# Four gated attention layers: shared expert in loops, no padding chunks, one dispatch buffer filled ahead, loads of SyncE reordered

## The reference

```python
x = x + tanh(g_xattn[l]) * attention_l(layernorm(x), ctx, ctx)
x = x + tanh(g_ffn[l]) * ffn_l(layernorm(x))   # layers 0 to 3
```

## Time and profile before

| | us |
|---|---|
| median of 3 runs | 2857.65 |
| lowest and highest of them | 2852.08, 2864.13 |
| the profiled execution | 2859.82 |
| its span in the trace | 2858.0 |

### The profile page before, as it was taken

The page is one execution under the profiler, slowest core; times in us unless marked ns, Lnnn a source line. Parts: engine busy times, 40 slices in busy tenths (PEclk is TensorE's granted clock), DMA queues, the critical chain, the costliest instruction groups (busy, mean ns, idle before and its releaser), DMA issues. The chain is left out here.

```text
span 2858.0 us, 66667 instructions
## 1 busy us (share of the span) xinstructions
PE 2314.3 (81%) x24114; PEld 1670.9 (58%) x24114; DVE 1598.7 (56%) x4258; ACT 1438.7 (50%) x2187; POOL 976.3 (34%) x1058
## 2 busy tenths in 40 slices
PE   6887774359999489889999998999969887159993
PEld 3554543249898255556777775555535554159982
DVE  5788886234444378852222222799968988413333
ACT  4665652123333277764454544777757666024441
POOL 4447774504444222211000000122112455734545
PEclk8999985679999799989999999999989999579996
DMA  3322221126666244430000000333313333157777
GB/s 87 104 76 82 77 84 52 38 74 207 203 206 180 81 119 118 117 91 13 0 0 0 0 0 1 94 103 103 109 56 91 95 104 95 59 161 218 231 219 229
DMA packets 183495, 284.19 MB, mean 99 GB/s; under 512 B 29177, under 2 KB 104449, under 8 KB 182722
## 3 DMA queue, kind: packets, MB, share of 16 engines
q1 hardware_dynamic: 119506, 122.36, 16.3%
q10 hardware_dynamic: 46480, 122.88, 13.1%
q0 software_dynamic: 17280, 35.95, 3.7%
HBM read 188.53 MB, written 76.91 MB: 93 GB/s over the span
## 5 line engine op out<-in xcount | busy, mean ns | idle before, releaser
L1798 DVE TENSOR_REDUCE mx<-psS 128x16 f32<-128x1024 f32 x264 | 322.2, 1221 | 197.5 <-PE psS L1297 190.3
L744 POOL DMA_INDIRECT yg<-ysb,yidx x284 | 276.1, 972 | 412.9 <-DVE ysb L2245 220.9
L1297 PE MATMUL psS<-kexp,qT 64*64 64x512 f32 x2112 | 297.2, 633 | 51.3 <-DVE work L1800 31.3
L1306 PEld LDWEIGHTS psT<-ident,work 128*128 128x128 f32 x2080 | 241.3, 147 | 166.3 <-ACT work L854 78.2
L854 ACT ACTIVATE work<-work 128x1024 f32<-128x1024 f32 x264 | 278.0, 1053 | 112.4 <-DVE work L1800 89.3
L860 ACT ACTIVATE work<-psT 128x1024 f32<-128x1024 f32 x260 | 265.4, 1021 | 127.3 <-PE psT L1306 122.0
L1800 DVE TENSOR_TENSOR work<-psS,mx 128x1024 f32<-128x1024 f32 x264 | 323.2, 1224 | 9.1
L1306 PE MATMUL psT<-ident,work 128*128 128x128 f32 x2080 | 291.4, 285 | 26.8 <-ACT work L854 12.9
L540 POOL TENSOR_TENSOR ve<-mv,eps 128x4 f32<-128x4 f32 x85 | 17.2, 202 | 818.0 <-DVE mv L1734 817.4
L1653 PEld LDWEIGHTS psY<-w_ffn,work 128*128 128x128 f32 x1988 | 243.9, 192 | 10.2 <-DVE work L2222 1.9
L1653 PE MATMUL psY<-w_ffn,work 128*128 128x128 f32 x1988 | 245.2, 275 | 2.0 <-DVE ysb L2245 1.4
(11 more groups left out here) (259 smaller groups left out, 4437.8 us busy)
## 6 DMA issues: line engine op xcount, KB each, us to landing
w_ffn<-in_wmoe ACTq DMA_DIRECT2D x71, 578.0 KB
w_ffn<-in_wmoe ACTq DMA_DIRECT2D x71, 576.0 KB
rawd<-raw ACTq DMA_DIRECT2D x64, 512.0 KB
vsum<-rawd SPq DMA_DIRECT2D x128, 256.0 KB
xin<-xg SPq DMA_DIRECT2D x142, 132.0 KB
ctxT<-in_ctxT SPq DMA_DIRECT2D x72, 256.0 KB
kexp<-kT SPq DMA_DIRECT2D x1144, 16.0 KB
gio<-yg SPq DMA_DIRECT2D x16, 512.0 KB, 6.0
```

The source lines that it names most:

```text
L744: e.indirect_dma_start(out=yg, out_offset=bass.IndirectOffsetOnAxis(ap=yidx[:, b, t:t + 1], axis=0), in_=ysb[:, b, t, :], in_offset=None, ...
L1297: m = e.matmul(psS[64 * half:64 * half + 64, 512 * k:512 * k + 512], qT[64 * k:64 * k + 64, b, c:c + SEQ], kexp[64 * k:64 * k + 64, b, :, ...
L1306: m = e.transpose(psT[:, r * P:(r + 1) * P], sc[:, s % 2, 2 * r:2 * r + 2, :].rearrange("p a b -> p (a b)"), ident[:, :])
L1798: e.tensor_reduce(mx[:, :], src, AX, ALU.max).then_inc(s_max, 1)
```

## The change

1. The shared expert runs as two chunks, a loop of six passes of two chunks, and two chunks, on PE, ACT and DVE. In the loop DVE's mean, scale and x slices have addresses from the loop register.
2. Chunks past the end are gone: NP, NK, NS and NT fall away, and a helper returns early.
3. `xg` is split in `xg[0]` and `xg[3]`. All regions of `xg[3]` are filled with padding rows by `prefill`, which SP issues behind barrier 3; the eight pad writes ahead of the experts of layer 3 are gone, and POOL waits for the fill before it scatters in attention 3. ACT's first 1056 KB pad write is made for each buffer.
4. On SP `y_load(None, 2)` of attention 1 stands ahead of `spread_k(1, None, 1)`; the 2048 KB weights of feed-forward 1 come in four loads, one behind each of the last four turns; `spread_k(1, None, 0)` moves from ahead of barrier 1 to the end of `experts(0)`.

```diff
+        def past(i, u):
+            return i is None and u >= CHUNKS
...
             def spread_k(lay, i, u):
+                if past(i, u):
+                    return
...
             def shift(lay, i, u, s):
+                if past(i, u):
+                    return
...
-                if lay in (0, 1):
-                    load_ffn(lay)
+                    load(wsh, a["wffn0"], wffn_in)
                 if lay in (1, 2):
                     weights_kv(lay + 1)
-                if lay == 1:
-                    y_load(None, 2)
...
+                if lay == 1:
+                    y_load(None, 2)
                 spread_k(lay, None, 1)
...
                 for u in range(CHUNKS - 4, CHUNKS):
                     turn(None, u)
+                    if lay == 1:
+                        load_ffn(u - (CHUNKS - 4))
...
+            def prefill():
+
+                for x in range(E):
+                    pad = a["pads"][x * SLOT:(x + 1) * SLOT, :].rearrange("(a p) d -> a p d", a=1)
+                    sp.dma_start(xg[3][x * REGION:(x + 1) * REGION, :].rearrange("(a p) d -> a p d", p=SLOT),
+                                 pad.broadcast_to([REGION // SLOT, SLOT, XW])).then_inc(pad_done, 16)
+
             def experts(lay):
                 m = MO[lay]
                 sp.wait_ge(m["tab"], 1)
-                for x in range(E):
-                    row = sp.value_load(padrow[0:1, x:x + 1], min_val=0, max_val=XROWS - SLOT)
-                    sp.dma_start(xg[bass.ds(row, SLOT), :], a["pads"][x * SLOT:(x + 1) * SLOT, :]).then_inc(pad_done, 16)
-                sp.wait_ge(pad_done, 16 * E * (1 + lay // 3))
+                if lay == 0:
+                    for x in range(E):
+                        row = sp.value_load(padrow[0:1, x:x + 1], min_val=0, max_val=XROWS - SLOT)
+                        sp.dma_start(xg[0][bass.ds(row, SLOT), :], a["pads"][x * SLOT:(x + 1) * SLOT, :]).then_inc(pad_done, 16)
+                    sp.wait_ge(pad_done, 16 * E)
...
                 for j in range(NB):
                     rows_in(j)
+                if lay == 0:
+                    spread_k(1, None, 0)
...
-            spread_k(1, None, 0)
             barrier(sp, 1)
...
             masks(None, 1)
+            prefill()
             barrier(sp, 4)
...
+                turn_in(None, 0)
+                turn_in(None, 1)
+                up(None, 0)
+                turn(None, 0)
+                turn(None, 1)
+                with e.Fori(0, (CHUNKS - 4) // 2) as i:
+                    turn(i, 2)
+                    turn(i, 3)
+                turn(None, CHUNKS - 2)
+                turn(None, CHUNKS - 1)
```

More of the change, by code:

```diff
@@ L276, in qbase @@
         def qbase(lay):
-            return NP * sum(QUSES[:lay]) + (lay + 1 if lay else 0)
+            return CHUNKS * sum(QUSES[:lay])
         def ahead(u, s, by):
@@ L774, in _ @@
             e.wait_ge(first_in, 16 * N_FIRST)
-            e.dma_start(xg[E * REGION:, :], a["pads"][E * SLOT:, :]).then_inc(zero_done, 16)
+            for lay in (0, 3):
+                e.dma_start(xg[lay][E * REGION:, :], a["pads"][E * SLOT:, :]).then_inc(zero_done, 16)
             e.activation(tg[:, :], tg[:, :], ACT.Tanh).then_inc(setup, 1)
             def xt(ph, i, u):
-                n = val(i, u, 1, ph * NP + 1)
+                n = val(i, u, 1, LNB[ph] + 1)
                 e.wait_ge(xt_ps, n)
@@ L985, in turn @@
                             q_out(lay, i, u + 1)
-                        if s == 3 and u + 2 <= CHUNKS:
+                        if s == 3 and u + 2 < CHUNKS:
                             xt(ATT[lay], i, u + 2)
@@ L1596, in down, with turn @@
                     m.then_inc(sd_ps, 1)
-                turn_in(0)
-                turn_in(1)
-                up(0)
-                for c in range(CHUNKS):
-                    if c + 2 < CHUNKS:
-                        turn_in(c + 2)
-                    if c + 1 < CHUNKS:
-                        up(c + 1)
-                    down(c)
+                def turn(i, c):
+                    if i is not None or c + 2 < CHUNKS:
+                        turn_in(i, c + 2)
+                    if i is not None or c + 1 < CHUNKS:
+                        up(i, c + 1)
+                    down(i, c)
+                turn_in(None, 0)
+                turn_in(None, 1)
+                up(None, 0)
+                turn(None, 0)
+                turn(None, 1)
+                with e.Fori(0, (CHUNKS - 4) // 2) as i:
+                    turn(i, 2)
+                    turn(i, 3)
+                turn(None, CHUNKS - 2)
+                turn(None, CHUNKS - 1)
             def experts(lay):
@@ L1849, in turn @@
                 def turn(i, u):
-                    more = i is not None or u + 2 <= CHUNKS
+                    more = i is not None or u + 2 < CHUNKS
                     for s in range(LT):
@@ L1942, in turn @@
                                 to8(i, u)
-                        if s == 2 and u + 2 <= CHUNKS:
+                        if s == 2 and u + 2 < CHUNKS:
                             ln_apply(ATT[lay], i, u + 2)
@@ L2157, in add, with turn @@
                                            ALU.mult, ALU.add).then_inc(su_x, 1)
-                rows_in(0)
-                rows_in(1)
-                for c in range(CHUNKS):
-                    if c + 2 < CHUNKS:
-                        rows_in(c + 2)
-                    mul(c)
-                    if c >= 1:
-                        add(c - 1)
-                add(CHUNKS - 1)
+                def turn(i, c):
+                    if i is not None or c + 2 < CHUNKS:
+                        rows_in(i, c + 2)
+                    mul(i, c)
+                    if i is not None or c >= 1:
+                        add(i, c - 1)
@@ L2169, in block_table @@
+                rows_in(None, 0)
+                rows_in(None, 1)
+                turn(None, 0)
+                turn(None, 1)
+                with e.Fori(0, (CHUNKS - 4) // 2) as i:
+                    turn(i, 2)
+                    turn(i, 3)
+                turn(None, CHUNKS - 2)
+                turn(None, CHUNKS - 1)
+                add(None, CHUNKS - 1)
             def block_table(lay):
```

206 lines of the change are left out of this document (120 added, 86 removed).

## The result

The kernel after takes 2810.55 us in the median of four runs (2805.07 to 2815.07), the kernel before beside it 2856.24. The ratio is 0.983, with a 95% interval of 0.9806 to 0.9854: 1.7% faster. The forecast was 2805, with a range of 2786 to 2832.

The account below looks back on a forecast made before the run. No engine bounds the whole span; the bound changes by stage and the change acts at the seams and shared expert. Terms 10 + 9.3 + 13 + 4 + 4 + 5 + 9.5 - 2 = 52.8 us gave 2805, range 2786 to 2832.

Parts of the forecast that it names:

- Attention 0: 10 taken: Tail of attention 0: without the padding chunk, the vsum load and everything up to barrier 0 come 10 us earlier, bounds 4 and 11.
- the raw of the last chunk moves from 440.43 to about 434 to 436: Tail of attention 0: without DVE's padding passes, 1.22 us each, the last raw comes at about 434 to 436.
- Barrier 1: 9.3 taken: Barrier 1: moving SP's 16 layer 1 spreads behind the experts opens it 9.3 us sooner, bounds 8.5 and 10.
- Loops: a loss of 2 taken: Shared expert as loops: a loss of 2 us for register work and branches, bounds 0 and 6; the stall stays.
- rival A: Shared expert: loops cure the stall under POOL's scatters, 48 us more gained, 2757 us; chance 0.10.
- Rival C: Shared expert: PE, ACT and DVE refetch code in each of six loop passes, 24 us, giving 2829; chance 0.03.
- Attention 1: 13 + 4 taken: Attention 1: 13 us from the early y load at its start, 4 us from padding passes gone in its tail.
- Attention 2: 4 taken: Tail of attention 2: padding passes gone ahead of the last raw, 4 us gained, bounds 2.5 and 7.
- Attention 3: 5 taken: Tail of attention 3: POOL's norm comes earlier, so its closing chain does, 5 us gained, bounds 3 and 8.
- Experts 3: 9.5 taken: Start of experts 3: SP's eight pad writes gone, 9.5 us gained, bounds 8 and 12; ACT's weights then set the start.
- The fill: 0 taken: Prefill behind barrier 3: 35.7 MB in 262 to 274 us, covered by layer 1's feed-forward, cost 0.
- rival D: Prefill outlasts its cover and delays attention 2's spreads; slower than before needs 543 us; 2878 at half rate; chance 0.04.

Follow-up runs that it names:

- e5: Kernel before, with SP leaving out only the spreads of the padding chunks, which are still computed on old keys; 2846.13 us, ratio 0.9953.
- e11: Kernel before, with DVE's passes over the padding score tiles cut to one head; 2780.61 us on the third chip, ratio 0.9993.
- e3: Kernel before, with only SP's new order: early y load, weights in four loads, layer 1 spreads behind the experts; 2843.06 us, ratio 0.9937.
- e1: Kernel after, with the shared expert unrolled again, and by the same edit attention 1 on PE, ACT, DVE and POOL; 2811.32 us, ratio 0.9844.
- e8: Kernel before, with only attention 1's y load of chunk 2 moved ahead of the spreads of chunk 1; 2770.71 us on the third chip, ratio 0.9952.
- e2: Kernel after, with loops, fill and load order taken back, so only the padding chunks are gone; attention 1's loops also unrolled; 2838.37 us, ratio 0.9927.
- e6: Kernel after, with 48 unused 128x128 transposes added on PE in the last three turns of attention 2; 2798.65 us, ratio 0.9783.
- e4: Kernel after, without the fill of the second buffer; the eight pad writes ahead of layer 3's experts are back; 2820.68 us, ratio 0.9878.
- e9: Kernel after, with 48 unused transposes on PE in attention 2's tail and more PE work at three other seams; 2728.09 us, ratio 0.9801.
- e7: Kernel after, with POOL's 48 scatters behind barrier 0 held until DVE has ended the shared expert; 2817.91 us, ratio 0.9844.
- e10: Kernel after, with 48 unused matmuls of 8 columns added on PE in the last three turns of attention 2; 2737.9 us, ratio 0.9844.

## Why the prediction was right, point by point

**Attention 0: 10 taken, 20.0 and 18.6 measured.** The direction was right, the term was half of what came, over its upper bound of 11, and the step that failed is "the raw of the last chunk moves from 440.43 to about 434 to 436". It moved by 16 us. I took DVE's two passes for the order-setting work and counted one block of spreads. e5 gives what the spreads are worth behind the last raw, 4.6 us, and 1.4 ahead of it; e11 says that DVE's passes alone are worth nothing that can be seen. The remaining 13 or so are other work of the padding chunks, or what only falls away when all of it goes; I had not costed it.

**Barrier 1: 9.3 taken; with the loops 10.4 and 11.3.** e3 has 10.7 for the spreads alone. The new place behind experts 0 was free: that stage is no longer than before.

**Loops: a loss of 2 taken, none seen** (e1). The stall was kept, as forecast, and rival A (the loops cure it) fell: the kernel after stands with loops as well, and in e8 the unrolled code runs at 3 us a chunk under the scatters. Rival C, the refetch, fell too: PE's last matmul comes 55.3 and 54.4 us behind barrier 0 with loops on the third chip, 55.6 and 54.2 without. By the rule of the Trainium skill, page "Runtime: NRT & Kernel Launch", section "Instruction fetch mechanics", a taken branch outside the window costs a fetch; the loops of this kernel show no such time (113.0 and 112.1 us with, 112.4 without).

**Attention 1: 13 + 4 taken, 22.2 and 23.7 measured.** The y load gave its 13 to 14 (e8). The rest of the stage gave 6.4 in e2 and some 8 in the whole change, not 4: for the same reason as in attention 0, the work of the padding chunks was more than the passes.

**Attention 2: 4 taken, 3.1 and 4.3 measured from barrier 4 to barrier 5.** Right.

**Attention 3: 5 taken, a loss of 4.7 and 2.4 measured.** This is the term with the wrong sign. The tail gave 9, but the chunks ahead of it became 12 to 14 us longer, in every kernel without padding on the first two chips but e6 (e1 7, e2 12, e4 18, e6 4). I had written that nothing of the change reaches the steady part. The trace puts the loss at ACT's wait for `vsum`, 10.5 us where it was 1.4, behind a store of `raw` that a packet of instructions on q8 holds up by some 2 us. I had read q8's 138 packets as too few to matter; their sum is, the place where they fall is not. e6 gets most of the loss back, with no such packet on its stores; e9, with the same work for PE on another chip, doesn't. That the missing padding moved the fetches is argued, not tried.

**Experts 3: 9.5 taken, about 7 at the start of the stage and about 4 over the whole of it.** The pads went as forecast. The first expert matmul, expected 7 to 8 us behind the barrier, came at 11.3. I had let it wait for ACT's weights more than for the rows; in the profile it stands behind the second block of rows, which is 5.16 us late. Later late blocks take more of it back. In the profile of the result the stage gave nothing, and the 9 us between the medians of e4 and e1 aren't the stage alone.

**The fill: 0 taken, 0 measured.** It takes 125 us of a cover of 473, from its issue at 1238 to barrier 4 (I worked out 262 to 274), so rival D, which needed 543, was far off. The pace of one 1056 KB write and of small packets was the wrong base: the fill went in packets of some 25 KB, and neither figure told its rate.

The sum of 52.8 against 46 to 51 thus rests on errors of opposite sign: attention 0 and attention 1 gave some 15 us more, barrier 1 and the loops some 3 more, attention 3 gave 7 to 10 less, and experts 3 gave 5 less by the mean of the profiles and 9 or more less in the two of the kernel after. That they met so near the forecast is luck.

## What to carry to other kernels

Work on padding at the end of a pipeline must be costed on every engine that it passes, projections, evictions and rotations too, and not only on the engine that looks busiest. A load that waits for nothing belongs ahead of a block of issues in its queue: one line moved brought 13 us. An edit made by its text should be checked for every place it hit, as in e1 and e2. Where a transfer is late for no reason in its own queue, the instruction queues are worth a look at that moment, whatever their share of the span. And a stage should be looked at on more than one chip before its stalls are put down to the code.

## What the runs showed of the hardware that was not expected

- The same shared expert beside the same scatters took 123.4 us (before) and 71.0 us (e8) on two chips; PE was busy 13.78 of 57 us on the one and 45.50 of 48 on the other. All runs on two chips, and the first pair, have the stall; the four on the third don't. What differs between them is open.
- With 48 indirect writes of 0.97 us and 0.30 between two in POOL's queue, ACT stood up to 23.94 us with "remote" as releaser. With the writes held back no such wait over 5 us was left (e7), nor was there one with the writes running on the third chip.
- With PE busy 5.99 of 6 us, nearly all of it in matmuls with 8 columns, the granted clock stood at its lower level, 0.50 (e10). With transposes of 128 columns at the same place it stood at 0.84 and 1.00, with PE busy 4.08 and 3.44 of 6 us (e9).
- 35.7 MB written from DRAM to DRAM in eight transfers ran at about 300 GB/s beside a full PE, and feed-forward 1 was no longer for it (478.9 us, before 479.5).
- Of 168 stores of 512 KB in attention 3, 58 ended more than 3.5 us behind their issue (up to 5.1, where most others took 2.4 to 3.1), and on 55 of the 58 lay a 16 KB packet of instructions (q8, 0.9 to 2.0 us long). Such late stores raised ACT's waits from 1.4 to 10.5 us in the kernel after, though q8 is 0.4% of the DMA time of the span.
